# Attentional factorization machine tower on one Trainium2 core: the low part of each step's last chunk made by two DMAs

## The chip, the cores and the metric

The kernel runs on 1 core of one Trainium2 chip. The metric is the device time of one execution in microseconds; the time of a kernel is the median of its runs. Engines are named as in the profile: PE (matmul, with PEld for its weight loads), DVE (vector), ACT (scalar), POOL (GpSimd) and SP (the queue that issues most DMAs). Each engine works off its own instruction stream in order, and semaphores tie the streams together.

## The reference, cut to what matters

```
row, col = np.triu_indices(33, k=1)                      # 528 pairs of 33 fields
e     = stack([tbl_f[ids[:, f]] for f in range(33)], 1)  # (1024, 33, 128)
inner = e[:, row] * e[:, col]                            # (1024, 528, 128)
fm    = relu(einsum('bpd,ad->bpa', inner, attn_W) + attn_b)
scores = einsum('ba,bpa->bp', gnn, fm)
attn   = softmax(scores, axis=1)
pooled = einsum('bp,bpd->bd', attn, inner) * 100.0
h = concat([gnn, pooled, gnn], axis=1)
y = relu(relu(h @ W_top1 + b_top1) @ W_top2 + b_top2) @ W_top3
```

All of it is float32.

## The kernel before, in words

The 1024 samples are worked off in 8 tiles (T) of 128. A tile is 32 steps (STEPS) of 4 samples; a step S, of 256 in all (ALL), has 4 x 528 = 2112 columns (COLS) of products, with the 128 embedding dimensions on the partitions.

For every step DVE forms the products of the field pairs (`product`, L405, tile `inner`), and PE multiplies them by the attention weights (`hidden`, L534 to L543) into PSUM in 5 chunks of 416 or 424 columns. A chunk is done in one of two ways. A native chunk (L534) is a float32 matmul, which runs as two passes. A split chunk takes three matmuls in the faster format float32r: ACT has rounded the products (`round_inner`, L298, `inner_hi`), DVE has subtracted the rounded from the exact ones (`rest_of_inner`, L412, `inner_lo`), and PE adds up low weights times high products, high weights times low products, high weights times high products (L541 to L543). The list NATIVE says how many of a step's chunks, from the first on, are native: 2 in steps 2, 5, 8, 11, 14 and 17 of each tile, 1 in the others, 4 and 3 in the first two steps of all.

ACT adds the bias and applies the relu while it takes two chunks at a time out of PSUM (`relu`, L290, `fm`). After every even step PE turns the two steps before into scores (`reduce_steps`, L564). `inner` and `inner_hi` have three buffers, `inner_lo` two, and PSUM gives three double banks to a ring (`ring`) that all units of PE's work share.

Other work of a tile lies between the steps, at places written out by hand: row maximum, exponential, scaling and transposing of the attention weights of the tile before (steps 1 to 4: L426, L305, L313, L439); the weighted sum over pairs in four parts c = 0 to 3 at steps 7, 10, 13 and 16 (FIELDS_AT; `fields`, L592, then `weigh` L447 and `sum_weighted` L454 on DVE); the transposes of the next tile's embedding rows at steps 18, 20, 22, 24 and 26 (XT_AT; `transpose_x`, L574, taken out of PSUM by ACT, L328); the three layers at steps 19, 21 and 23 (MLP_AT).

POOL gathers the embedding rows, one indirect DMA for each of 33 fields and tile (L259), as soon as the last tile's rows have been transposed and stored. SP stores a tile's rows in DRAM (`store_rows`, L213), and for each part c loads them back turned, with fields on the partitions (`load_fields`, L202, 4 DMAs into `x_fields`), and spreads the attention weights into a block diagonal (`spread_attn`, L207, 4 DMAs into `attn_t`); both tiles have two buffers, so that part c + 1 is loaded while part c is used. In the last tile ACT and DVE spread the weights themselves and parts 2 and 3 have buffers of their own.

These lines tie the low part to its buffers: PE waits for it once in a step, and DVE's product waits until it has been taken.

```
dve.wait_ge(s_lo, S - INNER_BUFS + 1)                                         # product
dve.wait_ge(s_hidden, CHUNKS * (S - INNER_BUFS) + NATIVE[S - INNER_BUFS])     # product
dve.wait_ge(s_hidden, CHUNKS * (S - LO_BUFS + 1))                             # rest_of_inner
pe.wait_ge(s_lo, S + 1)                                                       # hidden, first split chunk
```

Of the kernel before, what the change touches and what calls it, by code (L numbers as in the profile page):

```python
# [12 lines left out]
def afm_tower(nc, gnn, ids, tables, w1, b1, w2, b2, w3, attn_w, attn_b, out):  # L13
    P = 128
# [30 lines left out]
    SPLIT = COLS - THIN  # L45
    INNER_BUFS, HI_BUFS, LO_BUFS, FM_BUFS = 3, 3, 2, 3
    RING = 3
# [4 lines left out]
    MAX_AT, EXP_AT, INV_AT, SCALE_AT, TURN_AT = 1, 2, 2, 3, 4  # L52
# [21 lines left out]
    with ctx:  # L74
# [13 lines left out]
        inner_hi = sb("inner_hi", [D, HI_BUFS, SPLIT], FP32R)  # L88
        inner_lo = sb("inner_lo", [D, LO_BUFS, SPLIT], FP32R)
# [4 lines left out]
        x_fields = sb("x_fields", [P, 2, FN, D])  # L94
# [3 lines left out]
        attn_t = sb("attn_t", [P, 2, QS, FN, I])  # L98
# [7 lines left out]
        attn_wt_lo = sb("attn_wt_lo", [D, P], FP32R)  # L106
# [3 lines left out]
        h1 = sb("h1", [P, M1, P])  # L110
        h2 = sb("h2", [P, M2, P])
        y_row = sb("y_row", [1, P])
# [6 lines left out]
        gnn_rows = x_fields[:, 0, 0:T, :]  # L119
        attn_w_rows = x_fields[:, 1, 0, :]  # L120
        weighted = attn[:].rearrange("p a b -> p (a b)").rearrange("p (b f) -> p b f", f=I)
        TAIL_INNER = (ALL - 3) % INNER_BUFS
        attn_t_tail = inner[:, TAIL_INNER, 0:2 * QS * FN * I].rearrange("p (c q n i) -> p c q n i", c=2, q=QS, n=FN)
        x_fields_tail = x_rows[:, 0:2 * FN, :].rearrange("p (c n) d -> p c n d", c=2)
# [10 lines left out]
        s_fields = [sem(f"fields_loaded{i}") for i in range(2)]  # L135
# [6 lines left out]
        s_setup = sem("setup_copied")  # L142
        s_blocks = sem("gnn_blocks_written")
        s_inner = sem("inner_ready")
        s_hi = sem("inner_hi_ready")
        s_lo = sem("inner_lo_ready")
        s_hidden = sem("hidden_ready")
# [7 lines left out]
        s_spread = [sem(f"attn_t_written{i}") for i in range(2)]  # L155
        s_tail_zero = sem("tail_attn_t_zeroed")
        s_tail_attn = sem("tail_attn_t_written")
# [39 lines left out]
        def _(sp):  # L197
# [6 lines left out]
            def spread_attn(c):  # L204
                for q in range(QS):
                    own = slice(q * I, (q + 1) * I)
                    sp.dma_start(attn_t[own, c % 2, q], attn_turned[own, c * FN:(c + 1) * FN, :])\  # L207
                        .then_inc(s_spread[c % 2], 16)
# [17 lines left out]
            store_rows(1)  # L226
            sp.wait_ge(s_setup_t, 2)
            sp.wait_ge(s_store, 16)
            load_fields(0, 0, x_fields[:, 0], s_fields[0])
            load_fields(0, 1, x_fields[:, 1], s_fields[1])  # L230
            for t in range(T - 1):
                sp.wait_ge(s_inv, 3 * (t + 1))
                spread_attn(0)
                spread_attn(1)
                for c in (2, 3):
                    sp.wait_ge(s_fields_done, FJ * t + c - 1)
                    load_fields(t, c, x_fields[:, c % 2], s_fields[c % 2])
                    spread_attn(c)
                if t + 2 < T:
                    store_rows(t + 2)  # L240
                sp.wait_ge(s_store, 16 * (t + 2))
                for c in (0, 1):
                    sp.wait_ge(s_fields_done, FJ * t + c + 3)
                    load_fields(t + 1, c, x_fields[:, c], s_fields[c])
            sp.wait_ge(s_store, 16 * T)
            sp.wait_ge(s_xt_done, XJ * T)
# [5 lines left out]
        def _(pool):  # L252
# [17 lines left out]
            for t in range(T):  # L270
                gather(t)
# [406 lines left out]
```

## Time and profile before

| | |
|---|---|
| median of 3 runs | 1276.63 us (1275.88 to 1276.68) |
| the profiled execution | 1274.65 us |
| its span, first to last instruction | 1272.7 us |
| mean granted TensorE clock | 0.999 |
| DMA, over the span | 58.47 MB, 46 GB/s |

The profile is of one execution. A busy share is the time in which an engine had an instruction running, over the span. Matmuls are pipelined, so the lengths of single matmuls overlap; the time from the start of one block to the start of the same block two steps later is the better measure of PE's pace. The number behind `<-` in a row names what ended the idle time ahead of the instruction.

### The profile page before, as it was taken

The numbers are of one execution on the slowest core, as the hardware profiler recorded it, in microseconds if no ns is written. First come the engines' busy times: TensorE is split into PE (matmuls) and PEld (weight loads), VectorE is DVE, ScalarE is ACT, GpSimd is POOL, SyncE is SP. The second block draws the span as 40 slices with busy tenths as digits, with TensorE's granted clock in tenths as the row PEclk, the third lists the DMA queues.
The fourth block names the chain that finished last, engine by engine and source line by source line (L and its number), as shares of the span: only waits on it lengthen the run. The fifth ranks groups of instructions, "written<-read, shape, count | busy, mean of one in ns | idle before, by whom it ended". The sixth has DMA issues, their size and how long they took to land.

```text
span 1272.7 us, 21264 instructions
## 1 busy us (share of the span) xinstructions
PE 1208.2 (95%) x8752; PEld 903.2 (71%) x8752; DVE 1150.1 (90%) x643; ACT 1045.2 (82%) x1038; POOL 473.1 (37%) x271
## 2 busy tenths in 40 slices
PE   1499999999999999999999999999999999999998
PEld 1277776777777777777767777677776777677777
DVE  2499899998999989998999989999899998999974
ACT  2388999789887898879987799878988799887882
POOL 6586784018810487006840088202880000000000
PEclk9999999999999999999999999999999999999999
DMA  4212310311103101131102211031111300012100
GB/s 105 101 35 81 72 31 26 110 38 28 33 27 115 32 26 30 30 107 37 30 23 73 77 30 30 20 110 41 28 34 32 106 18 1 1 30 59 29 1 1
DMA packets 54288, 58.47 MB, mean 46 GB/s; under 512 B 10537, under 2 KB 48561, under 8 KB 53169
## 3 DMA queue, kind: packets, MB, share of 16 engines
q1 hardware_dynamic: 45728, 39.81, 10.5%
q0 software_dynamic: 8448, 17.32, 5.2%
q8 instruction: 69, 1.13, 0.4%
q14 instruction: 27, 0.21, 0.1%
q10 hardware_dynamic: 16, 0.00, 0.0%
HBM read 36.12 MB, written 17.31 MB: 42 GB/s over the span
## 4 chain that ended last, share of the span: by engine, by line
PE 77%; ACT 7%; issue 7%; DVE 6%; POOL 2%; DMA 0%; DVEq 0%; ACTq 0%; POOLq 0%
PE scores L564 18%; PE ring L534 16%; PE ring L541 12%; PE ring L542 11%; PE ring L543 11%; ACT fm L290 3%; PE ring L592 3%; DVE inner L405 3%; ACT inner_hi L298 3%; POOL x_rows L259 2%; PE ring L574 2%; DVE inner_lo L412 2%; PE ring L610 1%; DVE attn L447 1%; PE scores L621 1%
## 5 line engine op out<-in xcount | busy, mean ns | idle before, releaser
L290 ACT ACTIVATE fm<-ring,attn_b_sb 128x848 f32<-128x848 f32 (+1 forms) x640 | 597.3, 972 | 158.5 <-PE ring L534 152.2
L405 DVE TENSOR_TENSOR inner<-xt 128x2112 f32<-128x2112 f32 x256 | 602.2, 2353 | 64.9 <-ACT xt L328 35.1
L259 POOL DMA_INDIRECT x_rows<-in_tbl,ids_all x264 | 470.6, 1782 | 484.3 <-PE ring L574 394.5
L412 DVE TENSOR_TENSOR inner_lo<-inner,inner_hi 128x1688 fp32r<-128x1688 f32 (+4 forms) x256 | 466.8, 1823 | 26.1 <-ACT inner_hi L298 22.9
L541 PE MATMUL ring<-inner_hi,attn_wt_lo 128*128 128x424 f32 (+1 forms) x971 | 434.2, 447 | 4.7 <-ACT fm L290 4.0
L298 ACT CAST inner_hi<-inner 128x1688 fp32r<-128x1688 f32 (+4 forms) x256 | 392.4, 1533 | 5.2 <-DVE inner L405 5.2
L542 PE MATMUL ring<-inner_lo,attn_wt_hi 128*128 128x424 f32 (+1 forms) x971 | 344.1, 354 | 0.0
L543 PE MATMUL ring<-inner_hi,attn_wt_hi 128*128 128x424 f32 (+1 forms) x971 | 344.1, 354 | 0.0
L534 PE MATMUL ring<-inner,attn_wt 128*128 128x424 f32 (+1 forms) x618 | 275.6, 542 | 8.2 <-issue 4.5
L564 PE MATMUL scores<-fm,gnn_blocks 128*32 128x264 f32 x4096 | 254.6, 389 | 5.5 <-ACT exp_pairs L305 5.5
L541 PEld LDWEIGHTS ring<-inner_hi,attn_wt_lo 128*128 128x128 f32 x971 | 182.7, 188 | 72.4 <-issue 38.8
L542 PEld LDWEIGHTS ring<-inner_lo,attn_wt_hi 128*128 128x128 f32 x971 | 183.2, 189 | 43.3 <-issue 40.1
L564 PEld LDWEIGHTS scores<-fm,gnn_blocks 128*32 128x32 f32 x4096 | 119.9, 109 | 107.2 <-ACT fm L290 14.2
L543 PEld LDWEIGHTS ring<-inner_hi,attn_wt_hi 128*128 128x128 f32 x971 | 182.4, 188 | 5.4
L534 PEld LDWEIGHTS ring<-inner,attn_wt 128*128 128x128 f32 x618 | 104.6, 190 | 83.4 <-issue 74.7
L274 POOL MEMSET inner<- 128x2048 f32 x1 | 1.8, 1815 | 276.3 <-PE ring L543 276.3
L328 ACT COPY xt<-ring 128x1024 f32<-128x1024 f32 (+1 forms) x40 | 67.4, 1690 | 25.8 <-PE ring L574 25.8
L574 PE MATMUL ring<-ident,x_rows 128*128 128x128 f32 x264 | 39.2, 292 | 34.4 <-DMA x_rows<-in_tbl,ids_all 31.6
L574 PEld LDWEIGHTS ring<-ident,x_rows 128*128 128x128 f32 x264 | 33.0, 151 | 40.0 <-DMA x_rows<-in_tbl,ids_all 25.7
L592 PE MATMUL ring<-attn_t,x_fields 128*128 128x128 f32 x480 | 58.2, 275 | 0.0
L592 PEld LDWEIGHTS ring<-attn_t,x_fields 128*128 128x128 f32 x480 | 58.0, 191 | 0.3
L447 DVE TENSOR_TENSOR attn<-ring,xt 128x1024 f32<-128x1024 f32 x32 | 38.9, 1216 | 3.6 <-PE ring L592 3.3
(50 smaller groups left out, 253.2 us busy)
## 6 DMA issues: line engine op xcount, KB each, us to landing
x_dram<-x_rows SPq DMA_DIRECT2D x8, 2112.0 KB, 6.6
x_fields<-x_dram SPq DMA_DIRECT2D x120, 128.0 KB, 3.0
x_rows<-in_tbl,ids_all POOLq DMA_INDIRECT x264, 3.4
attn_t<-attn_turned SPq DMA_DIRECT2D x112, 32.0 KB, 1.9
w_sb<-in_W_top SPq DMA_DIRECT2D x2, 512.0 KB, 5.9
x_rows<-x_dram SPq DMA_DIRECT2D x8, 128.0 KB, 4.1
x_fields<-in_r_gnn_feature SPq DMA_DIRECT2D x1, 512.0 KB, 4.0
h<-in_W_top SPq DMA_DIRECT2D x1, 256.0 KB, 6.2
```

The costliest lines, as they stand in the source:

```text
L259: nc.gpsimd.indirect_dma_start(out=x_rows[:, f, :], out_offset=None, in_=tables[f], in_offset=bass.IndirectOffsetOnAxis(ap=ids_all[:, t, f ...
L290: nc.scalar.activation(dst, slot(("hidden", pair, j))[:, :, 0:n], ACT.Relu, bias=attn_b_sb[:, 0:1]).then_inc(s_fm, 1)
L298: nc.scalar.copy(inner_hi[:, S % HI_BUFS, 0:COLS - at], inner[:, S % INNER_BUFS, at:]).then_inc(s_hi, 1)
L405: nc.vector.tensor_tensor(dst, a, b, ALU.mult).then_inc(s_inner, 1)
L412: nc.vector.tensor_tensor(inner_lo[:, S % LO_BUFS, 0:COLS - at], inner[:, S % INNER_BUFS, at:], inner_hi[:, S % HI_BUFS, 0:COLS - at].bitc ...
L534: nc.tensor.matmul(dst, attn_wt[:], inner[:, S % INNER_BUFS, begin:end], start=True, stop=True)\
L541: nc.tensor.matmul(dst, attn_wt_lo[:], hi, start=True, stop=False)
L542: nc.tensor.matmul(dst, attn_wt_hi[:], lo, start=False, stop=False)
L543: nc.tensor.matmul(dst, attn_wt_hi[:], hi, start=False, stop=True).then_inc(s_hidden, 1)
L564: last = nc.tensor.matmul(scores[I * j:I * j + I, h, 0:HALF], block_of(s, j), fm[:, S % FM_BUFS, at:at + HALF], start=s == 0, stop=s == ST ...
L574: last = nc.tensor.transpose(to[:, n // 4, n % 4 * P:(n % 4 + 1) * P], x_rows[:, FU * c + n, :], ident[:])
L592: last = nc.tensor.matmul(bank[:, h, to:to + QS * I], x[:, n, :], own[:, :, n, :], start=True, stop=True)
```

## The change

The low part of the last chunk of each step (columns 1696 or 1688 to 2112) is no longer subtracted on DVE. SP copies these columns of the product into a tile of its own, `inner_lo_dma` with three buffers, and POOL issues a second DMA that adds the rounded columns onto the copy. For the sum to be the low part, rounding yields the negative of the rounded product (ACT's copy becomes an activation with scale -1), DVE's subtraction becomes an addition, and two of the three weights are negated. PE waits for the added columns ahead of a split last chunk.

The native chunks are dealt out anew: 1 in a step, 0 in steps 20, 22, 24, 26, 28 and 30 of a tile, all 5 in the first two steps of all, which therefore have no rounding and no low part. POOL's gathers for the next tile are dealt out over steps from five before the tile on (one or two in a step), between the additions. SP's work is ordered by step: the copy for step S + 3 comes first, then what is due of stores, spreads and loads. `x_fields` and `attn_t` have one buffer in place of two, so a part's loads are issued once the part before has been used. `h1`, `h2` and `y_row` lie in the tile `attn`. In the last tile the spread weights of all four parts lie in `inner` and the rows of parts 1 to 3 in `x_rows`, loaded from step 18 on.

```diff
-    NATIVE_2 = (2, 5, 8, 11, 14, 17)
-    NATIVE = [2 if S % STEPS in NATIVE_2 else 1 for S in range(ALL)]
-    NATIVE[0], NATIVE[1] = 4, 3
+    NATIVE_0 = (20, 22, 24, 26, 28, 30)
+    NATIVE = [0 if S % STEPS in NATIVE_0 else 1 for S in range(ALL)]
+    FIRST = 2
+    for S in range(FIRST):
+        NATIVE[S] = CHUNKS
+    LAST = CHUNKS - 1
+    DMA_BUFS = 3
+    SPREAD_AT = 5
+    STORE_AT = 18
+    def gathers_of(S):
+        t, s = divmod(S + 5, STEPS)
+        return t + 1, [f for f in range(F) if f * 2 // 3 == s] if t + 1 < T else []
...
+        def split_step(S):
+            return S - FIRST + 1
+        def dma_turn(S):
+            return 16 * len(range(S, FIRST - 1, -DMA_BUFS))
+        def dma_cols(S):
+            return EDGES[S % 2][LAST], EDGES[S % 2][LAST + 1]
...
+            def copy_inner(S):
+                sp.wait_ge(s_inner, S + 1)
+                if S >= FIRST + DMA_BUFS:
+                    sp.wait_ge(s_hidden, CHUNKS * (S - DMA_BUFS + 1))
+                begin, end = dma_cols(S)
+                sp.dma_start(inner_lo_dma[:, S % DMA_BUFS, 0:end - begin].bitcast(FP32),
+                             inner[:, S % INNER_BUFS, begin:end]).then_inc(s_copied[S % DMA_BUFS], 16)
...
+            load_fields(0, 0, x_fields[:], s_fields)
+            copy_inner(FIRST)
+            for S in range(ALL):
+                t, s = divmod(S, STEPS)
+                if S + 3 < ALL:
+                    copy_inner(S + 3)
+                if s == STORE_AT and t + 1 < T:
+                    store_rows(t + 1)
+                if s == SPREAD_AT and t > 0:
+                    sp.wait_ge(s_inv, 3 * t)
+                    spread_attn(0)
+                for c in range(FJ):
+                    if s == FIELDS_AT[c] + 1 and t > 0:
+                        sp.wait_ge(s_fields_done, FJ * (t - 1) + c + 1)
+                        if c + 1 < FJ:
+                            spread_attn(c + 1)
+                            load_fields(t - 1, c + 1, x_fields[:], s_fields)
+                        else:
+                            sp.wait_ge(s_store, 16 * (t + 1))
+                            load_fields(t, 0, x_fields[:], s_fields)
+                if t == T - 1 and s == STORE_AT:
+                    for c in range(1, FJ):
+                        load_fields(T - 1, c, x_fields_tail[:, c], s_fields_tail)
...
+            def take_off_hi(S):
+                pool.wait_ge(s_hi, split_step(S))
+                pool.wait_ge(s_copied[S % DMA_BUFS], dma_turn(S))
+                begin, end = dma_cols(S)
+                nc.gpsimd.dma_start(inner_lo_dma[:, S % DMA_BUFS, 0:end - begin].bitcast(FP32),
+                                    inner_hi[:, S % HI_BUFS, begin:end].bitcast(FP32), accum_op=ALU.add)\
+                    .then_inc(s_added[S % DMA_BUFS], 16)
...
-            for t in range(T):
-                gather(t)
+            for f in range(F):
+                gather(0, f)
+            for S in range(-5, ALL):
+                if 0 <= S and S + 2 < ALL:
+                    take_off_hi(S + 2)
+                t, some = gathers_of(S)
+                for f in some:
+                    gather(t, f)
...
-                nc.scalar.copy(inner_hi[:, S % HI_BUFS, 0:COLS - at], inner[:, S % INNER_BUFS, at:]).then_inc(s_hi, 1)
+                nc.scalar.activation(inner_hi[:, S % HI_BUFS, at:], inner[:, S % INNER_BUFS, at:], ACT.Copy, scale=-1.0)\
+                    .then_inc(s_hi, 1)
...
             def product(S):
+                if S >= FIRST + INNER_BUFS:
+                    dve.wait_ge(s_lo, split_step(S - INNER_BUFS))
+                    dve.wait_ge(s_copied[S % DMA_BUFS], dma_turn(S - INNER_BUFS))
                 if S >= INNER_BUFS:
-                    dve.wait_ge(s_lo, S - INNER_BUFS + 1)
                     dve.wait_ge(s_hidden, CHUNKS * (S - INNER_BUFS) + NATIVE[S - INNER_BUFS])
...
-                at = native_cols(S)
-                nc.vector.tensor_tensor(inner_lo[:, S % LO_BUFS, 0:COLS - at], inner[:, S % INNER_BUFS, at:],
-                                        inner_hi[:, S % HI_BUFS, 0:COLS - at].bitcast(FP32), ALU.subtract).then_inc(s_lo, 1)
+                at, end = native_cols(S), EDGES[S % 2][LAST]
+                nc.vector.tensor_tensor(inner_lo[:, S % LO_BUFS, at:end], inner[:, S % INNER_BUFS, at:end],
+                                        inner_hi[:, S % HI_BUFS, at:end].bitcast(FP32), ALU.add).then_inc(s_lo, 1)
...
+                    if c < LAST:
+                        lo = inner_lo[:, S % LO_BUFS, begin:end]
+                    else:
+                        pe.wait_ge(s_added[S % DMA_BUFS], dma_turn(S))
+                        lo = inner_lo_dma[:, S % DMA_BUFS, 0:end - begin]
+                    nc.tensor.matmul(dst, attn_wt_lo_neg[:], hi, start=True, stop=False)
                     nc.tensor.matmul(dst, attn_wt_hi[:], lo, start=False, stop=False)
+                    nc.tensor.matmul(dst, attn_wt_hi_neg[:], hi, start=False, stop=True).then_inc(s_hidden, 1)
```

## Rows read from the trace of the kernel before

**Rows 1.** The page: busy time, share and instructions of each engine.
```profile
PE 1208.2 (95%) x8752; PEld 903.2 (71%) x8752; DVE 1150.1 (90%) x643; ACT 1045.2 (82%) x1038; POOL 473.1 (37%) x271
L259 POOL DMA_INDIRECT x_rows<-in_tbl,ids_all x264 | 470.6, 1782 | 484.3 <-PE ring L574 394.5
```

**Rows 2.** Windows of tile 3: steps 2-6, 7-17, 18-23; length, then busy us.
```profile
501.04:524.27 23.23, 21.95 (x165) 15.14 (x165) 23.02 (x17) 21.53 (x23) 3.52 (x2) 1.00 0.07 18
524.27:576.47 52.20, 52.12 (x378) 39.80 (x375) 51.53 (x30) 38.44 (x37) 0.00 (x0) 1.00 0.28 88
576.47:609.18 32.71, 31.98 (x242) 24.54 (x240) 28.28 (x16) 32.55 (x35) 24.82 (x12) 1.00 0.09 23
```

**Rows 3.** The chain that ended last, tile 0: starts of the scores blocks, one per pair.
```profile
90.59 1.92 PE scores L564 x32
98.73 1.92 PE scores L564 x32
107.01 1.92 PE scores L564 x32
```

**Rows 4.** Groups by line and shape: busy us, mean ns, idle before.
```profile
L412 DVE TENSOR_TENSOR inner_lo<-inner,inner_hi 128x1696 fp32r<-128x1696 f32 x103 | 197.8, 1921 | 5.4 <-ACT inner_hi L298 2.2
L298 ACT CAST inner_hi<-inner 128x1696 fp32r<-128x1696 f32 x103 | 165.0, 1602 | 0.3 <-DVE inner L405 0.3
L412 DVE TENSOR_TENSOR inner_lo<-inner,inner_hi 128x1272 fp32r<-128x1272 f32 x24 | 35.4, 1475 | 0.0
L298 ACT CAST inner_hi<-inner 128x1272 fp32r<-128x1272 f32 x24 | 29.9, 1248 | 0.0
```

**Rows 5.** Waits over the span: engine, line, releaser, us in total, times, longest.
```profile
PEld ring L541 <- DVE attn L447: 5.5, 14, 0.5
```

**Rows 6.** Timeline of ACT around steps 18 to 23 of tile 3: start, length.
```profile
579.10 1.62 ACT L298 CAST inner_hi<-inner 128x1688 fp32r<-128x1688 f32 x1
...
610.74 0.97 ACT L290 ACTIVATE fm<-ring,attn_b_sb 128x848 f32<-128x848 f32 x1 [0.72 <-PE ring L543]
```

**Rows 7.** POOL's gathers: shortest, median, longest ns; then landing after issue.
```profile
L259 POOL DMA_INDIRECT x_rows<-in_tbl,ids_all x264: 941/1744/3135, 4.6 to 953.8; - x132
...
DMA to landing us min/median/max: 2.4/3.4/4.7
```

**Rows 8.** Timeline of DVE and POOL in tile 1: two gathers beside DVE.
```profile
287.89 2.35 DVE L405 TENSOR_TENSOR inner<-xt 128x2112 f32<-128x2112 f32 x1
289.09 1.96 POOL L259 DMA_INDIRECT x_rows<-in_tbl,ids_all  x1 [0.30 <-issue]
291.35 0.94 POOL L259 DMA_INDIRECT x_rows<-in_tbl,ids_all  x1 [0.30 <-issue]
291.41 1.92 DVE L412 TENSOR_TENSOR inner_lo<-inner,inner_hi 128x1688 fp32r<-128x1688 f32 x1 [1.18 <-ACT inner_hi L298]
```

**Rows 9.** Timeline of the start: PE's first step, POOL's gathers for tile 1.
```profile
53.15 4.99 PE L534 MATMUL ring<-inner,attn_wt 128*128 128x424 f32 x8 [4.51 <-issue]
55.02 1.11 POOL L259 DMA_INDIRECT x_rows<-in_tbl,ids_all  x1 [8.86 <-DMA x_dram<-x_rows]
...
67.71 0.96 PE L534 MATMUL ring<-inner,attn_wt 128*128 128x416 f32 x2
...
70.18 1.53 POOL L259 DMA_INDIRECT x_rows<-in_tbl,ids_all  x1 [0.30 <-issue]
```

**Rows 10.** Windows of the end; the last three columns: clock, DMA, GB/s.
```profile
1242.80:1244.80 2.00, 0.00 (x0) 0.00 (x0) 0.71 (x1) 1.22 (x2) 0.00 (x0) 1.00 0.00 0
1244.80:1248.20 3.40, 3.34 (x8) 2.62 (x9) 2.08 (x3) 1.18 (x3) 0.00 (x0) 0.50 0.00 0
```

**Rows 11.** SP's issues of the spread weights: shortest, median, longest ns.
```profile
L207 SPq DMA_DIRECT2D attn_t<-attn_turned x112: 512/590/1815, 214.1 to 1148.2; - x112
```

**Rows 12.** SP's loads of the field rows: ns of an issue; the page: landing.
```profile
L202 SPq DMA_DIRECT2D x_fields<-x_dram x120: 303/451/1292, 123.5 to 1174.4; - x120
x_fields<-x_dram SPq DMA_DIRECT2D x120, 128.0 KB, 3.0
```

More of the change, by code:

```diff
@@ L116, in afm_tower @@
         inv_sum = sb("inv_sum", [P, 1])
[L119 to L124, printed above, removed]
+        gnn_rows = x_fields[:, 0:T, :]
+        attn_w_rows = attn_turned[:, 0:D // I, :].rearrange("p n i -> p (n i)")
+        spare = attn[:].rearrange("p a b -> p (a b)")
+        weighted = spare.rearrange("p (b f) -> p b f", f=I)
+        h1 = spare[:, 0:H1].rearrange("p (m b) -> p m b", b=P)
+        h2 = spare[:, H1:H1 + H2].rearrange("p (m b) -> p m b", b=P)
+        y_row = spare[0:1, H1 + H2:H1 + H2 + P]
+        assert {S % INNER_BUFS for S in (ALL - 3, ALL - 2)} == {1, 2}
+        attn_t_tail = inner[:, 1:3, :].rearrange("p r n -> p (r n)")[:, 0:FJ * QS * FN * I]\
+            .rearrange("p (c q n i) -> p c q n i", c=FJ, q=QS, n=FN)
+        x_fields_tail = x_rows[:, 0:FJ * FN, :].rearrange("p (c n) d -> p c n d", c=FJ)
         ring = [pb(f"ring{i}", [P, 2, 512]) for i in range(RING)]
@@ L134, in afm_tower @@
         s_store = sem("rows_stored")
-        s_fields = [sem(f"fields_loaded{i}") for i in range(2)]
+        s_fields = sem("fields_loaded")
         s_fields_tail = sem("tail_fields_loaded")
@@ L146, in afm_tower @@
         s_lo = sem("inner_lo_ready")
+        s_copied = [sem(f"inner_copied{i}") for i in range(DMA_BUFS)]
+        s_added = [sem(f"inner_hi_taken_off{i}") for i in range(DMA_BUFS)]
         s_hidden = sem("hidden_ready")
@@ L154, in afm_tower @@
         s_attn = sem("attn_scaled")
-        s_spread = [sem(f"attn_t_written{i}") for i in range(2)]
+        s_spread = sem("attn_t_written")
         s_tail_zero = sem("tail_attn_t_zeroed")
-        s_tail_attn = sem("tail_attn_t_written")
+        s_tail_attn = [sem(f"tail_attn_t_written{i}") for i in range(2)]
         s_fields_done = sem("fields_filled")
@@ L225, in _ @@
             store_rows(0)
-            store_rows(1)
             sp.wait_ge(s_setup_t, 2)
             sp.wait_ge(s_store, 16)
[L229 to L246, printed above, removed]
-            load_fields(T - 1, 2, x_fields_tail[:, 0], s_fields_tail)
-            load_fields(T - 1, 3, x_fields_tail[:, 1], s_fields_tail)
+            load_fields(0, 0, x_fields[:], s_fields)
[21 more added lines that the diff above has]
+                        load_fields(T - 1, c, x_fields_tail[:, c], s_fields_tail)
             sp.wait_ge(s_out, 16 * T)
@@ L349, in _ @@
             nc.scalar.copy(attn_wt_hi[:], attn_wt[:]).then_inc(s_setup, 1)
+            nc.scalar.activation(attn_wt_hi_neg[:], attn_wt[:], ACT.Copy, scale=-1.0).then_inc(s_wt_neg, 1)
             for c in range(XJ):
@@ L476, in _ @@
             product(1)
-            rest_of_inner(0)
             product(2)
```

117 lines of the change are left out of this document (54 added, 63 removed).

## Prediction

> **What bounds the kernel now.** I read the busy shares first, then the stages of one middle tile, then the waits. PE is busy 95% of the span, DVE 90%, ACT 82%, POOL 37% [rows 1]; the reader should see that three engines are close together, so a gain on one is soon met by the next. The windows of tile 3 say where [rows 2]. In steps 7 to 17 (52.20 us) PE works 52.12 and DVE 51.53. In steps 2 to 6 (23.23 us) DVE works 23.02 and PE 21.95. In steps 18 to 23 (32.71 us) ACT works 32.55 and PE 31.98. PE sets the pace nearly everywhere, with ACT equal to it while the next tile is transposed and DVE equal to it early in the tile. What can be won is mostly PE's own work.
>
> **PE: fewer native chunks.** A native chunk is two float32 passes, a split chunk three short ones. The starts of the scores blocks give the price: the pair of steps with two native chunks in all lasted 98.73 - 90.59 = 8.14 us, the next, with three, 107.01 - 98.73 = 8.28 [rows 3]; the pairs on either side repeat these two lengths. One native chunk more costs 0.14 us. Before has 38 native chunks a tile and 5 more in the first two steps, 309; after has 26 a tile and 8 more there, 216. (a) The six second native chunks of a tile go: 48 x 0.14 = -6.7. (b) Six even steps (20 to 30) lose their only one. That takes the change of weights out of the step too, which no row shows; bounds 0.14 and 0.20, I take 0.17. Three of the six lie in the stretch where ACT sets the pace in the tiles that transpose a next one (7 of 8) and give nothing there: 48 - 21 = 27 x 0.17 = -4.6.
>
> **DVE** subtracts 1272 columns in place of 1696 in 20 of 32 steps: 1.92 - 1.47 = 0.45 us each [rows 4], 9 us a tile, and keeps its 2.35 us product [rows 8]. Most of it only turns into idle time, since PE has the same length. What PE waited for DVE's weighting is 5.5 us in 14 waits [rows 5]; with DVE early I take (c) -4.5 (bounds 0 and -5.5).
>
> **ACT** rounds 2112 columns in place of 1696 in the steps 20 to 30 that are even, and 1696 in place of 1272 in the old two-native steps: 1.602 - 1.248 = 0.35 us for each 424 columns [rows 4]. In steps 7 to 17 ACT has gaps that cover it (38.44 us of work in 52.20 [rows 2]), but from step 18 on it has none until 610.7 [rows 6]. Three longer roundings fall in that stretch: up to 1.06 us a tile, less where PE was late as well; (d) 0.5 x 7 = +3.5 (bounds 0 and 7.4). Step 5's longer rounding stands ahead of the scaling of attn, behind which ACT's next two evacuations queue: (e) 7 x 0.35 = +2.5 (bounds 0 and 2.5). Rounding becomes an activation with a scale and the subtraction an addition; same columns, taken at nothing; 0.05 us more for each rounding would be hidden except in the ACT stretch (+0.3 a tile, inside (d)'s bound).
>
> **POOL and the two DMAs.** Per step SP copies 217 KB and POOL issues an accumulating DMA of the same size, 254 each. No row shows an accumulating DMA. The nearest are the gathers: 0.94 us of POOL at least, 1.74 median, 3.14 at most, landing 2.4 to 4.7 us after issue, median 3.4 [rows 7], plus 0.30 us between two. Why they spread is seen in [rows 8]: the gather of 289.09 ended 0.81 us after DVE's product did (287.89 + 2.35 = 290.24; 291.05), while the one of 291.35 took 0.94 although a DVE subtraction of two inputs ran over nearly all of it. So a gather is held once, at its start, while DVE runs; its remaining 0.8 us is not disturbed. A plain DMA has no index list to read, so I take 0.94 + 0.30 = 1.25 us (bounds 0.94 and 3.44) and 3.4 us to land.
> That is weighed against a rule of the Trainium skill. The page "SBUF — State Buffer", section "SBUF: two separate sides", warns that DMAs issued from GpSimd can starve while VectorE holds the shared port pair; it also says that an op with two SBUF inputs holds it only against a GpSimd op that reads SBUF. The row of 291.35 agrees with the second half. If the first half governed here, it would be the rival "POOL" below.
> POOL per pair of steps in the 22 steps with gathers: three gathers at 1.90 + 0.30 (the 231 gathers after the first 33 take 470.6 - 33 x 0.945 = 439 us [rows 1, 7]) and two adds at 1.25: 6.6 + 2.5 = 9.1 us, against 8.14 us for a pair without extra jobs [rows 3]. It fits only because a gather gets through at each of four DVE ends in a pair, and because the add is early: rounding for step S+2 is done 4.25 us after step S begins (579.10 + 1.62 - 576.47) [rows 2, 6], while PE wants the last chunk at 8.14 + 0.73 + 3 x 0.59 = 10.6 us (8.14 less 1.92 for scores leaves 6.2 for ten chunks, two of them native and 0.14 dearer: 0.59 a split one, 0.73 a native one, an estimate). 10.6 - 4.25 - 3.4 leaves 3.0 us, room for a queue of one gather. (f) 0 in the steady tile, 0 to +3 us a tile in the range.
>
> **The start.** POOL's program puts eight gathers of tile 1 ahead of the first add (step 2). They can't start before 55.02, when tile 0's rows are stored, and the same eight ended at 70.18 + 1.53 = 71.7 in the trace [rows 9]. DVE runs out of work there after its sixth product, so I take 70.5, add 1.25 and land at 74.0. PE would ask for that chunk at about 65.1: ten native chunks from 53.15, 10 x 0.73 = 7.3, and 2.1 more because four of them took 4.99 and not 2.9 at the start [rows 9]; then 2.5 for step 2's first four. It waits 8.9 us, and step 3, at 67.71 before [rows 9], begins at 74.0 + 0.6 + 1.9 = 76.5: +8.8. The clock adds to it: after 2.0 us without PE work the granted clock was 0.50 (1.2 GHz) for 3.4 us late in the trace [rows 10]; the half of 3.4 is 1.7. (g) +10.5 (bounds 7.5, a short add and no clock, and 12.5).
>
> **Single buffers.** The fields' loads for part c+1 are issued by SP only after part c is used, behind the step's copy and four spread DMAs at 0.59 us each [rows 11]; four loads at 0.45 follow, the last landing 3.0 us after issue [rows 12]. From the start of step 8: the copy waits for product 11 (3.7), + 0.5 + 2.3 + 1.3 + 3.0 = 10.8; PE wants them at 11.2 (steps 8, 9 and hidden of 10). A near tie, in 21 places: (h) +2.5 (bounds 0 and 10). Behind the late SP stands the next copy; the 3 us above cover it. The tail's copies are fewer before the first part, but the 12 filler matmuls end at the same time: 0.
>
> **Sum.** -6.7 - 4.6 - 4.5 + 3.5 + 2.5 + 0 + 10.5 + 2.5 = +3.2. The profiled execution took 1274.65 (span 1272.7 and 1.95 around it); the median of the three runs is 1276.63, 2 us above. On the median: **1280**.
>
> **Rivals.**
> *POOL becomes the bound (slower).* If the add too is held at its start until DVE ends, a pair needs five DVE ends and has four: 4 x 1.92 + 1.25 = 8.9 us, 0.8 over 8.14, in six pairs without jobs 4.8 us a tile, of which some 2 are covered: 7 x 2.8 = +20 with the sum above, about 1300. The same price holds if the add lands in over 6 us. It decides where POOL's five issues exceed the pair. At 2.2 us for each add they take 11.0 against 9.1 in 11 pairs, and the loss would be over 100 us; DVE's idle time when PE is late speaks against that. For it: no row of an accumulating DMA. Against: the row of 291.35.
> *PE's gain comes through whole (faster).* ACT's longer roundings and the reloads hide (d, e, h at 0), a native chunk at the even steps is worth 0.19 in all 48 places (-9.1), DVE's waits go whole, start +9: -6.7 - 9.1 - 5.5 + 9 = -12.3, about 1264. For it: ACT's shares outside one stretch. Against: [rows 6].
> *The start doesn't stall* would need the add ahead of the gathers; the program's order excludes it.
>
> **Chances.** Forecast 0.45 (own range 1271 to 1288), POOL or a late add 0.30, whole gain 0.25. The forecast's own range splits as 0.08 faster, 0.17 within, 0.20 slower, so: faster by over 0.2% 0.33, within 0.2% 0.17, slower 0.50; 0.2%, 2.6 us, is about what a measurement of this kernel can tell from no change. The range takes the whole-gain case's centre and most of the POOL case: 1264 to 1305.
>
> **What would show it.** Start: step 3 at 75 to 78 us and half clock there; if it stands at 68, (g) is wrong. Adds: POOL busy near 0.95 us each whatever DVE does; lengths like the gathers' make the POOL rival right. PE waiting on the added chunk in steps 27 to 6 means that (f) is wrong; a pair without jobs of 8.14 or less means it is right. Steps 18 to 23 longer than 32.7 confirm (d). PE waiting for x_fields confirms (h).

## The result and the profile after

The changed kernel ("after" below; the kernel before it is "before") takes 1316.75 us, the median of 4 runs (1311.78 to 1318.42), against 1276.66 for the kernel before: a ratio of 1.0308 with an interval of 1.0295 to 1.032. Forecast were 1280 and a range of 1264 to 1305. The direction was right; size and range were wrong. The direction was partly luck: of the +3.2 us forecast, +10.5 was the start, which measured less, and +2.5 the reload of the single buffers, which measured ten times as much. The profiled execution took 1311.78, its span is 1309.9, 37.2 us over the span of before.

The page of after, busy shares, the two kinds of POOL's work and the last-ending chain by line:

```profile
PE 1209.3 (92%) x8845; PEld 916.0 (70%) x8845; DVE 1091.1 (83%) x641; ACT 1074.0 (82%) x1037; POOL 669.2 (51%) x525
...
PE scores L614 15%; PE ring L591 10%; PE ring L592 9%; PE ring L593 9%; PE ring L580 9%; DMA x_fields<-x_dram 5%; PE ring L644 4%; ACT fm L340 4%; SPq L234 4%; DVE inner L455 4%; SPq L229 2%; PE ring L624 2%; ACT inner_hi L348 2%; DMA inner_lo_dma<-inner_hi 1%
...
L303 POOL DMA_DIRECT2D inner_lo_dma<-inner_hi x254 | 236.8, 932 | 515.0 <-ACT inner_hi L348 456.9
L294 POOL DMA_INDIRECT x_rows<-in_tbl,ids_all x264 | 432.0, 1636 | 91.2 <-issue 75.7
```

Against [rows 1], DVE has lost 59 us of work and POOL, the forecast's worry, stands at 51%. PE has as much work as before, in a longer span: it waits. What is new in the chain is a transfer, the field rows (`x_fields`, 5%), and SP's queue at the spread (L234, 4%) and load lines (L229, 2%).

The waits, engine, line and releaser, then us in total, times and the longest:

```profile
PE ring L644 <- DMA x_fields<-x_dram: 19.0, 19, 2.4
DVE attn L497 <- PE ring L644: 16.1, 11, 3.2
...
PE ring L591 <- DMA inner_lo_dma<-inner_hi: 7.8, 4, 5.2
```

PE's weighted sums, 28 in the middle tiles and the last, wait for their field rows 19 times; for a low part made by the DMAs it waits four times in 254.

The windows of tile 3, steps 2 to 6, 7 to 17 and 18 to 23, as in [rows 2]:

```profile
518.60:542.11 23.51, 21.79 (x167) 15.40 (x165) 22.78 (x18) 22.02 (x23) 17.27 (x13) 1.00 0.54 125
542.11:601.05 58.94, 53.70 (x382) 41.89 (x379) 48.76 (x29) 39.61 (x38) 40.68 (x29) 0.97 0.57 136
601.05:634.46 33.41, 32.05 (x243) 24.81 (x242) 26.27 (x16) 33.24 (x35) 5.82 (x7) 1.00 0.55 159
```

The first and last stretch are 0.28 and 0.70 us longer. The middle one, which holds the four weighted sums, is 6.74 longer, and PE's idle part of it went from 0.08 to 5.24. Tile 3 is the longest of tiles 1 to 7; in the others the middle stretch is 1.3 to 3.3 us longer than before. From the starts of PE's first product in each step, the whole 37.2 divides into: tiles 1 to 6, 153.4 to 158.2 us each where before has 150.4, together +25.7; tile 0, 147.8 against 138.9, +8.9; step 0 begins at 55.62 and not 53.15, +2.5; tile 7 +1.8; the tail -1.6.

**The middle stretch.** SP's timeline in steps 14 and 15 of tile 3 (step 14 begins at 578.71), then PE's of step 16: start, length, and in brackets the wait ahead.

```profile
582.43 0.47 SPq L241 DMA_DIRECT2D inner_lo_dma<-inner  x1
582.95 3.46 SPq L234 DMA_DIRECT2D attn_t<-attn_turned  x4
586.45 2.06 SPq L229 DMA_DIRECT2D x_fields<-x_dram  x4
...
589.74 0.34 PE L593 MATMUL ring<-inner_hi,attn_wt_hi_neg 128*128 128x416 f32 x1
592.33 3.61 PE L644 MATMUL ring<-attn_t,x_fields 128*128 128x128 f32 x16 [2.24 <-DMA x_fields<-x_dram]
595.87 1.99 PE L614 MATMUL scores<-fm,gnn_blocks 128*32 128x264 f32 x32
```
```profile
592.33:595.70 3.37, 3.37 (x16) 3.37 (x16) 0.45 (x1) 0.00 (x0) 3.07 (x3) 0.51 0.44 115
```

SP could have reloaded at about 578.9 (in the first experiment the same spread is issued 0.2 us into step 14), but the copy for step 17 is ahead in its queue and waits until 582.43 for DVE's product. The reload's eight issues then end at 588.51, the rows land by 592.33, and PE, ready at 590.1, waits. Step 16 of this tile is the longest of the 21 steps with a reload, 10.93 us for 6.80 before, for two more reasons: one spread issue took 1.55 us, and PE's 16 matmuls behind the wait ran at half pace (3.61 us, 1.95 in the first experiment), at a granted clock of 0.51, the lower of TensorE's two levels (1.2 GHz; the window shown last). In the profile that happened behind one of the 19 waits.

**The start.** PE and POOL around step 2 of tile 0:

```profile
67.47 0.35 PE L593 MATMUL ring<-inner_hi,attn_wt_hi_neg 128*128 128x424 f32 x1
73.07 0.69 PE L591 MATMUL ring<-inner_hi,attn_wt_lo_neg 128*128 128x416 f32 x1 [5.24 <-DMA inner_lo_dma<-inner_hi]
...
74.38 3.17 PE L614 MATMUL scores<-fm,gnn_blocks 128*32 128x264 f32 x32
77.47 0.97 PE L580 MATMUL ring<-inner,attn_wt 128*128 128x416 f32 x2
```
```profile
68.64 1.09 POOL L294 DMA_INDIRECT x_rows<-in_tbl,ids_all  x1 [0.30 <-issue]
69.72 1.01 POOL L303 DMA_DIRECT2D inner_lo_dma<-inner_hi  x1
```
```profile
73.00:76.40 3.40, 3.33 (x23) 1.81 (x27) 1.48 (x1) 0.00 (x0) 2.80 (x3) 0.50 0.64 148
```

The eight gathers end at 69.73, the first addition is issued behind them, PE has it 3.35 us later, and its next work runs at half pace (scores 3.17 against 1.92) at a granted clock of 0.50 (1.2 GHz; the window shown last). Step 3, at 67.71 in [rows 9], begins at 77.47; of these 9.76 us, 2.47 are the later start of step 0 and 7.29 the wait and the half pace.

### The profile page after: what moved, and what is told of

Read it like the earlier page. It is cut to its first block, busy times and chain, and to the rows that moved or that the text cites. A ratio compares the mean times of both kernels' runs of the same rounds, so it can differ in the third digit from the quotient of the medians.

```text
span 1309.9 us, 22775 instructions
## 1 busy us (share of the span) xinstructions
PE 1209.3 (92%) x8845; PEld 916.0 (70%) x8845; DVE 1091.1 (83%) x641; ACT 1074.0 (82%) x1037; POOL 669.2 (51%) x525
## 2 busy tenths in 40 slices
DMA packets 127450, 167.85 MB, mean 128 GB/s; under 512 B 18664, under 2 KB 121712, under 8 KB 126320
## 4 chain that ended last, share of the span: by engine, by line
PE 62%; ACT 9%; DMA 8%; SPq 7%; issue 6%; DVE 5%; another core or an unknown queue 1%; POOL 1%; ACTq 0%; DVEq 0%; POOLq 0%
PE scores L614 15%; PE ring L591 10%; PE ring L592 9%; PE ring L593 9%; PE ring L580 9%; DMA x_fields<-x_dram 5%; PE ring L644 4%; ACT fm L340 4%; SPq L234 4%; DVE inner L455 4%; SPq L229 2%; PE ring L624 2%; ACT inner_hi L348 2%; DMA inner_lo_dma<-inner_hi 1%
## 5 line engine op out<-in xcount | busy, mean ns | idle before, releaser
L303 POOL DMA_DIRECT2D inner_lo_dma<-inner_hi x254 | 236.8, 932 | 515.0 <-ACT inner_hi L348 456.9
L591 PE MATMUL ring<-inner_hi,attn_wt_lo_neg 128*128 128x424 f32 (+1 forms) x1064 | 457.5, 430 | 21.5 <-ACT fm L340 9.7
L462 DVE TENSOR_TENSOR inner_lo<-inner,inner_hi 128x1272 fp32r<-128x1272 f32 (+1 forms) x254 | 397.4, 1564 | 86.5 <-ACT inner_hi L348 77.5
L348 ACT ACTIVATE inner_hi<-inner 128x1688 fp32r<-128x1688 f32 (+1 forms) x254 | 428.7, 1688 | 0.8 <-DVE inner L455 0.8
L593 PE MATMUL ring<-inner_hi,attn_wt_hi_neg 128*128 128x424 f32 (+1 forms) x1064 | 377.1, 354 | 0.0
L592 PE MATMUL ring<-inner_lo,attn_wt_hi 128*128 128x424 f32 x810 | 287.8, 355 | 0.0
L591 PEld LDWEIGHTS ring<-inner_hi,attn_wt_lo_neg 128*128 128x128 f32 x1064 | 200.3, 188 | 92.4 <-issue 43.8
L580 PE MATMUL ring<-inner,attn_wt 128*128 128x416 f32 (+1 forms) x432 | 200.9, 551 | 7.4 <-issue 7.4
L593 PEld LDWEIGHTS ring<-inner_hi,attn_wt_hi_neg 128*128 128x128 f32 x1064 | 200.3, 188 | 5.0
L592 PE MATMUL ring<-inner_lo_dma,attn_wt_hi 128*128 128x416 f32 x254 | 89.9, 354 | 0.0
```

The source lines that it names most:

```text
L303: nc.gpsimd.dma_start(inner_lo_dma[:, S % DMA_BUFS, 0:end - begin].bitcast(FP32), inner_hi[:, S % HI_BUFS, begin:end].bitcast(FP32), accum ...
L348: nc.scalar.activation(inner_hi[:, S % HI_BUFS, at:], inner[:, S % INNER_BUFS, at:], ACT.Copy, scale=-1.0)\
L462: nc.vector.tensor_tensor(inner_lo[:, S % LO_BUFS, at:end], inner[:, S % INNER_BUFS, at:end], inner_hi[:, S % HI_BUFS, at:end].bitcast(FP3 ...
L580: nc.tensor.matmul(dst, attn_wt[:], inner[:, S % INNER_BUFS, begin:end], start=True, stop=True)\
L591: nc.tensor.matmul(dst, attn_wt_lo_neg[:], hi, start=True, stop=False)
L592: nc.tensor.matmul(dst, attn_wt_hi[:], lo, start=False, stop=False)
```

## The experiments

The theory after the result, "queue place": the reload is late because SP issues it behind a copy that waits for DVE, and the rest of the loss is the start. The rivals: the single buffer by itself, the traffic of the copies and additions, and POOL.

**SP's due reload ahead of the step's copy.**

```diff
-                if S + 3 < ALL:
-                    copy_inner(S + 3)
-                if s == STORE_AT and t + 1 < T:
-                    store_rows(t + 1)
                 if s == SPREAD_AT and t > 0:
...
                             load_fields(t, 0, x_fields[:], s_fields)
+                if S + 3 < ALL:
+                    copy_inner(S + 3)
+                if s == STORE_AT and t + 1 < T:
+                    store_rows(t + 1)
```

> The changed kernel, with SP's work of a step turned round: the spread weights and field rows that are due come ahead of the step's copy, not behind it. Steps 10, 13 and 16 are together 4.0 us longer in a middle tile of the changed kernel than in the kernel before (7.9 for 6.8, 6.3 for 4.9, 8.2 for 6.8). Theory 'queue place' (the loads are late because SP issues them behind a copy that waits 3.7 us for its product): these steps fall back to about 6.8, 4.9 and 6.8, 7 x 4.0 = 28 us less, about 1290 us, and no add comes late, since the copy has room. Rival 'DMA load' (the two new streams of DMAs slow the field rows down wherever they are issued): less than half of it, over 1303 us. Rival 'single buffer' (one buffer is too little whatever the order): the same, over 1303 us.

1290.17 us (1286.66 to 1296.52), ratio 1.0094 (1.0066 to 1.0121). Steps 10, 13 and 16 of tiles 1 to 7 fell to 6.88, 4.90 and 6.88 us, with all copies and additions still there; in after's profile they came to 26.5 more in all. The median fell by 26.6, but that the two agree so closely is chance, since this kernel's executions differ by 9.9 us. Queue place is shown. The profiled execution, the slowest of the four, has losses that nothing had foretold: tile 0 took 3.3 us more than in after, and step 7 of tiles 1 and 2 took 7.7 instead of 4.9. POOL, then DVE, then PE in tile 1:

```profile
231.29 9.35 POOL L294 DMA_INDIRECT x_rows<-in_tbl,ids_all  x1 [0.30 <-issue]
240.59 1.00 POOL L303 DMA_DIRECT2D inner_lo_dma<-inner_hi  x1
```
```profile
230.92 1.48 DVE L462 TENSOR_TENSOR inner_lo<-inner,inner_hi 128x1272 fp32r<-128x1272 f32 x1
232.30 2.37 DVE L455 TENSOR_TENSOR inner<-xt 128x2112 f32<-128x2112 f32 x1
234.56 1.50 DVE L462 TENSOR_TENSOR inner_lo<-inner,inner_hi 128x1272 fp32r<-128x1272 f32 x1
235.95 2.38 DVE L455 TENSOR_TENSOR inner<-xt 128x2112 f32<-128x2112 f32 x1
238.21 1.51 DVE L462 TENSOR_TENSOR inner_lo<-inner,inner_hi 128x1272 fp32r<-128x1272 f32 x1
239.72 2.36 DVE L455 TENSOR_TENSOR inner<-xt 128x2112 f32<-128x2112 f32 x1
```
```profile
243.85 0.46 PE L591 MATMUL ring<-inner_hi,attn_wt_lo_neg 128*128 128x424 f32 x1 [2.54 <-DMA inner_lo_dma<-inner_hi]
```

A gather lay 9.35 us on POOL while DVE went from one two-input instruction to the next without a gap; it ended 0.92 us after the first end behind which DVE's next one did not already overlap (239.72). Other long gathers came free at an end that the next instruction did overlap, so which end frees a gather isn't shown. The addition queued behind it was late, and PE waited. The addition itself took 1.00 us beside the next product.

**The first addition ahead of tile 1's gathers.**

```diff
-                if s == STORE_AT and t + 1 < T:
+                if s == (STORE_AT if t > 0 else 23) and t + 1 < T:
...
                 t, some = gathers_of(S)
+                if S < STEPS - 5:
+                    t, some = 1, [f for f in range(F) if f * 2 // 3 == S]
```

> The changed kernel, with the gathers for tile 1 dealt out from step 0 on (two for each three half steps, as for the other tiles, but five steps later) and tile 1's rows stored at step 23 in place of 18, so that no gather stands ahead of the first addition. Theory 'start' (step 2 waits for the addition that stands behind eight gathers): step 2, 12.64 us in the changed kernel, falls to about 5.5 and step 3 begins 7 us earlier, about 1309 us. Rival: the first addition is late because of the copy or the rounding; step 2 stays over 10 us, 1316 us.

1304.51 us (1302.28 to 1310.29), ratio 1.023 (1.0202 to 1.0258). Step 2 took 5.42 us instead of 12.64 and tile 0 140.07 instead of 147.8. The median is 12.2 us below after's, but its executions, like after's, differ by 7 to 8 us. The profiles say more: step 2 is 7.2 us shorter, step 20 1.1, and tile 0 as a whole 7.7.

**Both edits in one kernel.**

> Both edits. If the two losses are independent: 28 + 7 = 35 us less, about 1282 us, still 5 us over the kernel before, from ACT's longer roundings in steps 18 to 23 (0.7 us a tile), step 4 (0.35 a tile) and a start of step 0 that is 2.5 us later. If they overlap, 1290 or more.

1280.75 us (1278.72 to 1285.5), ratio 1.0036 (1.0019 to 1.0052). Tiles 1 to 6 last 150.3 to 150.7. In these tiles everything else in the change adds up to nearly nothing: before has 150.4. The median is still 3.6 us over the 1277.16 of before beside it.

**The kernel before with single-buffered fields and weights.** No copies, no additions.

```diff
-                    sp.dma_start(attn_t[own, c % 2, q], attn_turned[own, c * FN:(c + 1) * FN, :])\
-                        .then_inc(s_spread[c % 2], 16)
+                    sp.dma_start(attn_t[own, 0, q], attn_turned[own, c * FN:(c + 1) * FN, :])\
+                        .then_inc(s_spread[0], 16)
...
-                spread_attn(1)
-                for c in (2, 3):
-                    sp.wait_ge(s_fields_done, FJ * t + c - 1)
-                    load_fields(t, c, x_fields[:, c % 2], s_fields[c % 2])
+                for c in (1, 2, 3):
+                    sp.wait_ge(s_fields_done, FJ * t + c)
+                    spread_attn(c)
+                    load_fields(t, c, x_fields[:, 0], s_fields[0])
...
```

> The kernel before, with spread weights and field rows in one buffer only: part c + 1 is spread and loaded once part c is used (in the last tile parts 0 and 1 keep their two buffers). SP has no copies here. Theory 'queue place': the loads are issued as soon as part c is done, 8 issues take 4.2 us and the last lands 3 us later, 7.2 us, against some 8 us until the next part (two steps); 0 to 3 us slower, 1277 to 1280 us. Rival 'single buffer': as in the changed kernel, 20 us or more slower, over 1296 us.

1277.66 us (1276.65 to 1278.85), ratio 1.0003 (0.9994 to 1.0013); tiles 150.4 as before. The single buffer alone costs nothing. Its step 0 begins at 55.94, though, so the +2.5 us at the start is not the change's: it came in a kernel that has the old start. Before's profiled execution is the odd one: from first to last instruction it lasts 1272.7 us, the 15 executions of before taken beside this kernel 1274.7 to 1275.4.

**The steps without a native chunk moved out of ACT's full stretch**, on top of both edits.

```diff
-    NATIVE_0 = (20, 22, 24, 26, 28, 30)
+    NATIVE_0 = (6, 8, 12, 14, 26, 28)
```

> Both edits of the run before (reload ahead of the copy, first addition ahead of the gathers; 1280.75 us), and the six steps without a native chunk moved from 20, 22, 24, 26, 28, 30 to 6, 8, 12, 14, 26, 28: as many native chunks, but the longer roundings leave the stretch where ACT has no gap. Theory 'ACT': steps 18 to 23 fall from 33.4 us to about 32.7, as in the kernel before, 7 tiles x 0.7 = 5 us less, about 1276 us. Rival 'PE alone' (it doesn't matter where native chunks go, since PE sets the pace): 1280 to 1281 us.

1271.01 us (1269.35 to 1276.87), ratio 0.996 (0.9945 to 0.9976): it beats both kernels, by 0.4% the kernel before, and 5 us more than expected. (The first four kernels, the next four and the last three were measured apart from each other, with before beside them at 1277.16, 1276.96 and 1277.03.) The windows of tile 3, same steps as above:

```profile
502.28:525.80 23.52, 21.81 (x168) 15.60 (x166) 22.78 (x17) 22.37 (x23) 16.35 (x14) 1.00 0.56 129
525.80:576.89 51.09, 51.09 (x385) 40.84 (x382) 49.82 (x30) 40.69 (x38) 40.71 (x28) 1.00 0.69 162
576.89:609.56 32.67, 31.95 (x241) 24.55 (x241) 25.24 (x16) 32.51 (x35) 7.00 (x8) 1.00 0.52 150
```

The last stretch is back at the 32.7 of [rows 2], and the middle one is 1.1 shorter than before, with PE never idle. ACT's longer roundings cost nothing where ACT has gaps. Step 30, which has its native chunk back, also fell, from 5.26 on average to 5.10.

**Both edits, without the additions.** The low part of the last chunk is left as copied.

```diff
-                    take_off_hi(S + 2)
+                    pool.wait_ge(s_hi, split_step(S + 2))
...
-                        pe.wait_ge(s_added[S % DMA_BUFS], dma_turn(S))
+                        pe.wait_ge(s_copied[S % DMA_BUFS], dma_turn(S))
```

> Both edits of the run before, without POOL's additions: SP still copies, PE takes the copy as it is, so the low part of the last chunk is left unreduced. 54 MB of accumulating transfers and 254 issues on POOL are gone. Theory 'cover' (in the steady tile the additions lie wholly beside other work once the first is early): 1279 to 1281 us, tiles of 150.3 to 150.7 as with them. Rival 'the addition is late at times' or slows other transfers: over 3 us less, under 1278 us.

1276.38 us (1274.97 to 1276.86), ratio 0.999 (0.9981 to 1.0), 4.4 less than with them. So they are not quite covered, against (f). The profiled tiles hardly differ (150.3 to 150.4 against 150.3 to 150.7). What differs in them is step 30, 5.26 us on average with additions and 5.09 without: there PE reaches the last chunk before its addition has landed. Tile 0 is 1.2 us shorter without. The spread of the executions is 1.9 us here and 6.8 with additions; where the rest of the 4.4 lies isn't shown.

**ACT's scaling behind step 3's evacuations**, on the 1271.01 kernel, to win (e) back.

```diff
-                if s == SCALE_AT and t > 0:
-                    scale_attn(t - 1)
                 relu(S // 2, 3 if S % 2 else 1)
                 if S % 2:
                     relu(S // 2, 4)
+                if s == SCALE_AT and t > 0:
+                    scale_attn(t - 1)
```

> The kernel with native chunks moved, and on ACT in step 3 the scaling of attn behind the two relus of the step instead of ahead of them. Step 4 lasts 6.16 us in the changed kernel, 5.81 in the one before, 5.1 in tile 0, where nothing is scaled. Theory 'scaling' (PE waits in step 4 for PSUM banks that ACT empties only after the scaling): step 4 falls to 5.1 to 5.4, 7 x 0.8 = 5.6 us less than the kernel with native chunks moved, about 1270 us. Rival: the scaling then comes late for the turning and spreading of attn, and step 7 waits: the same time or longer.

1294.68 us (1287.36 to 1298.22), ratio 1.0154 (1.0137 to 1.0171): a miss. Step 4 fell from 6.16 to 5.09, but step 5 rose from 3.12 to 5.00 and step 8 from 4.99 to 5.33 on average, 1.1 us a tile lost. And in tile 3 step 12 took 11.85. POOL there, then PE:

```profile
540.30 7.21 POOL L294 DMA_INDIRECT x_rows<-in_tbl,ids_all  x1 [0.30 <-issue]
547.45 1.00 POOL L303 DMA_DIRECT2D inner_lo_dma<-inner_hi  x1
...
550.10 2.82 POOL L294 DMA_INDIRECT x_rows<-in_tbl,ids_all  x1 [0.30 <-issue]
552.90 1.03 POOL L303 DMA_DIRECT2D inner_lo_dma<-inner_hi  x1
```
```profile
558.81 0.69 PE L593 MATMUL ring<-inner_hi,attn_wt_lo_neg 128*128 128x416 f32 x1 [4.39 <-DMA inner_lo_dma<-inner_hi]
```

As in tile 1 of the first experiment, a gather is held and the additions behind it are late. The one that PE waits for is that of 552.90, with a second held gather just ahead of it; it also took 5.9 us to reach PE, where that of 240.59 took 3.3, and why is not shown. That made a new theory, "held gather", for the losses that the steps do not explain.

**Both edits, without either DMA**: DVE makes all low parts, native chunks as in after.

> Both edits of the run before, with the two DMAs undone: DVE makes the low part of all split chunks (1696 columns, 2112 in the six steps without a native chunk), SP keeps the waits of the copies without the copies, POOL only gathers; native chunks as in the changed kernel. Theory 'DVE' (the DMAs pay for the 93 native chunks that went: DVE, 134 us busy in a tile of 150, gets 14 us more and is back at PE's length): tiles of 151 to 155 us, 1285 to 1310 us. Rival 'PE alone' (DVE's relief was worth nothing): tiles of 150.5, 1280 us.

1295.13 us (1294.7 to 1295.62), ratio 1.0143 (1.0126 to 1.016); tiles 153.1. Without the DMAs the same native chunks cost 14.4 us more than with them: DVE is then without a gap (53.37 us of work in the 53.37 of steps 7 to 17), and steps 6, 8 and 14 take 5.9, 6.1 and 5.9 for 5.1, 5.0 and 5.0. It also shows the holding at its largest. The gathers, issue time shortest, median and longest in ns, of this kernel and then of after:

```profile
L290 POOL DMA_INDIRECT x_rows<-in_tbl,ids_all x264: 940/1960/16264, 4.3 to 1069.4; - x132
```
```profile
L294 POOL DMA_INDIRECT x_rows<-in_tbl,ids_all x264: 940/1400/3456, 4.5 to 1059.8; - x132
```

No addition is queued behind them here, and the executions lie within 0.9 us.

**The late scaling without the additions.** The edit is that of the two kernels together.

> The kernel of e7 without POOL's additions (the low part of the last chunk stays the copied product), so that nothing of PE's waits for POOL's queue in the steps. In e7 one gather of tile 3 lay 7.21 us on POOL and the additions behind it came late: PE waited 4.39 us in step 12. Theory 'held gather': e7's loss beyond the profile is such gathers, in other tiles in each execution; without additions 7 tiles at 1.1 us over e5 (150.5 against 149.4) on 1271.0 stay, 1278.7, or up to 4.4 us less, which the additions cost in e3: 1274 to 1279, and its executions lie within 2.5 us of each other. Rival 'ACT': the scaling behind step 3's evacuations makes the loss by itself: about 1288 to 1295.

1279.78 us (1278.01 to 1282.72), ratio 1.0021 (1.0011 to 1.003). Slightly over the range expected; 14.9 us of the loss went with the additions, though the longest gather lay 8.30 us on POOL. ACT as the cause of the large loss has fallen. The spread, 4.7 us, is more than the 2.5 expected. Gathers were still held, eight of them for over 4 us, and in the profile they cost something without any addition behind them: step 17 took 3.84 to 3.91 us in just the four tiles in which a gather of step 16 lay 4.7 us on POOL, and 3.27 in the others. By which wait is open.

**The late scaling with plain loads for gathers**, in tiles 1 to 7.

```diff
-                nc.gpsimd.indirect_dma_start(
-                    out=x_rows[:, f, :], out_offset=None, in_=tables[f],
-                    in_offset=bass.IndirectOffsetOnAxis(ap=ids_all[:, t, f:f + 1], axis=0),
-                ).then_inc(s_gather[c], 16)
+                if t == 0:
...
+                else:
+                    nc.gpsimd.dma_start(x_rows[:, f, :], tables[f][0:P, :]).then_inc(s_gather[c], 16)
```

> The kernel of e7 with the gathers of tiles 1 to 7 replaced by plain DMAs of 128 rows of the same table, issued by POOL at the same places (the choice of rows by ids is left out for these tiles). Additions stay. Theory 'held gather': a plain DMA is issued in 0.9 to 1.1 us like the additions, whatever DVE does; none lies over 2 us on POOL, no addition is late, and the time is 1273 to 1279 with executions within 2.5 us. Rival 'additions': the additions or POOL's queue as such are late when DVE is full, whatever kind of DMA stands between them: 1288 to 1295 as in e7. Rival 'ACT': the same 1288 to 1295.

1276.87 us (1275.13 to 1279.52), ratio 0.9999 (0.9989 to 1.0009): 17.8 less than with gathers, with all additions in place. The two groups on POOL, busy us and mean ns:

```profile
L306 POOL DMA_DIRECT2D inner_lo_dma<-inner_hi x254 | 220.2, 868 | 840.3 <-ACT inner_hi L353 654.1
...
L300 POOL DMA_DIRECT2D x_rows<-in_tbl x231 | 173.4, 846 | 2.0 <-issue 1.8
```

The longest of the 231 plain loads lay 0.954 us on POOL. Step 17 is 3.26 to 3.28 in every tile. So it is the gather that is held beside DVE's instructions, not POOL's DMAs as such, and it costs most where an addition stands behind it.

**The 1271.01 kernel with plain loads for gathers.** The same edit.

> The kernel of e5 with the gathers of tiles 1 to 7 replaced by plain DMAs of 128 rows of the same table (the choice of rows by ids is left out for these tiles). Theory 'held gather': e5's executions spread from 1269.35 to 1276.87 because a gather is held in some of them; with plain DMAs they lie within 2.5 us and the median is 1267 to 1270. Rival: the spread comes from the additions or the traffic itself and stays, with a median near 1271.

1269.27 us (1268.84 to 1272.53, 4 runs), ratio 0.9942 (0.9925 to 0.996). 1.7 us less than with gathers: in that kernel held gathers cost little in the median. Their intervals overlap, so this is no more than in line with the theory; a spread of 3.7 us stays, more than the 2.5 expected. Beside it the late scaling alone costs 7.6 us (1276.87), the 1.1 a tile that its steps show.

## Why the prediction was wrong, point by point

**The step that failed is (h), single buffers**: +2.5, with bounds 0 and 10, and it measured 26.5 in the profiles. The mechanism was named (loads behind the copy and the spreads in SP's queue, "a near tie, in 21 places") and the first experiment shows it. Its sum was 10.8 against 11.2 us; the 19 places in which PE waited for the rows measured 11.8 to 14.0, with PE ready at 11.4 to 11.6. The first spread was issued at 4.0 to 4.2, as said. The last load was issued at 8.4 to 8.6 in 15 of the 21 places and at 8.9 to 9.7 in six, where 7.8 was forecast: 24 of after's 112 spread issues took over 0.7 us (8 to 24 in the kernels with additions, 1 to 6 in those without). PE had the rows 3.2 to 4.3 us after that issue, where 3.0 came from a trace with little else on the rings [rows 12]: the DMAs move 58.47 MB in before and 167.85 in after. In the single-buffered kernel without copies and additions the last load of a part landed 3.05 us after issue in the median, in a later kernel that has both (the late scaling with plain loads) 3.4: in line with some 0.4 us from the added DMAs. Together the misses cost 1.3 us on average in each of 21 places. The upper bound failed because it was built on medians: one spread in four at the longest of [rows 11], 1.815 for 0.59, gives 10.8 + 1.2 - 11.2 = 0.8 us, 17 us in 21 places.

**(g), the start**: the mechanism was right, an addition queued behind eight gathers and half pace behind the wait, but +10.5 was too much. Step 3 at 77.47 looks like the 76.5 forecast by luck: step 0 began 2.47 us late, for another reason, and the wait and the half pace made 7.3 us, just under the lower bound of 7.5. What the forecast had not seen is step 20 of tile 0, where PE waits for an addition beside the store of tile 1's rows (2.1 MB, issued at 142.88); the experiment moved that store away as well.

```profile
143.16 0.86 POOL L303 DMA_DIRECT2D inner_lo_dma<-inner_hi  x1 [2.86 <-ACT inner_hi L348]
152.15 0.43 PE L591 MATMUL ring<-inner_hi,attn_wt_lo_neg 128*128 128x416 f32 x1 [1.98 <-DMA inner_lo_dma<-inner_hi]
```

This addition took 9.0 us from its issue to PE.

**Without (g) and (h)** the forecast's sum was -9.8 us, and it did not come either: in tiles 1 to 6 the steps other than 10, 13 and 16 last as long as before, to 0.1 us a tile. This is the second step that failed; the points below divide it.

**(a), (b), (c), PE's gains**: -15.8 us were forecast. (a) and (c) came to about 7 us of the 11.2: steps 5, 8 and 14 shortened by 0.14, 0.38 and 0.50 us, DVE's part of (c) among it; steps 2, 11 and 17 did not move in the tiles that have weighted sums. (b) came to nearly nothing: steps 26 and 28 shortened by 0.08 and 0.07, where 0.17 was taken and 0.14 the lower bound, step 24 by 0.13, and step 30 became 0.23 longer, since its last chunk waits for the addition (5.09 without additions). A scores pair with one native chunk more [rows 3] is not the price of the last one.

**(d), (e), ACT**: +0.5 a tile forecast, 0.7 measured in steps 18 to 23; step 4 is 6.16 and not 5.81, exactly the 0.35 of (e). Both were right. That (d) was avoidable is shown by the moved native chunks.

**(f) and the rival POOL**: after's additions take 0.835 to 1.072 us whatever DVE does, and up to 1.19 in the other kernels. The sign named for (f), a pair without jobs of 8.14 or less, was met by steps 28 and 29 (8.07) and missed by 26 and 27 (8.33) and by 30 and 31 (8.45 for 8.23 before). So the choice of the row of 291.35 in [rows 8] was right, 0 to 3 us a tile held, and the rival's own price did not come. But one step of the working was wrong, that "a gather gets through at each of four DVE ends". In [rows 2] steps 7 to 17 of before hold no gather at all (POOL 0.00, x0) and steps 2 to 6 two; nearly all rows of the gathers were from other stretches, and the change moves most of them into these two, where DVE is fullest in before. In before 211 of 213 held gathers came free at the first end of a DVE instruction, in after 134 of 143, in the kernel in which DVE has no gap 176 of 211, the others at the second to the eighth (held: over 1.3 us on POOL). In after none is held over 3.46 us, and none over 3.20 with the first addition alone put ahead. As soon as the reload was mended, gathers of 4.3 to 9.4 us appeared, in step 5, a stretch in which DVE has as much to do as in after (22.79 us of 23.53 in steps 2 to 6, 22.78 of 23.51 in after); why only then is open. Held gathers make the 15 to 18 us of the late scaling, and may be part of the 4.4 that the additions cost with both queues mended; that was not tried apart.

The Trainium skill, page "SBUF — State Buffer", section "Who interferes with whom", says that a VectorE instruction with two SBUF inputs contends with a GpSimd instruction that reads SBUF. These traces agree: the gather, which takes its row numbers from SBUF, is held and the plain load at the same places is not (up to 7.21 us against 0.954; 16.26 where DVE has no gap). They go further than the page's lock for the length of an instruction, since a train of such instructions kept a gather waiting past up to eight ends. The row of 291.35, which the prediction took for a gather that two inputs don't hold, doesn't show that: this gather began 0.06 us before the subtraction did (291.41).

**The rival "whole gain"** needed (d), (e) and (h) at nothing. With the queues mended and (d) avoided, the change gives -6.0 us (1271.01 against 1276.96 beside it), not -12.3; (e) is still in it.

## What to carry to other kernels

Where a buffer is halved, its reload is only as early as its place in the in-order queue that issues it: put what is due at once ahead of what still waits, and count a near tie at the price of a miss times the places. Before work is moved to another stretch, look whether the rows that price it lie in a stretch with the same engines as full; a count of x0 says that nothing is known there. Behind an instruction that can be held for many microseconds, here an indirect gather, queue nothing that the bounding engine needs soon.

## What the runs showed of the hardware

An accumulating DMA of 128 x 416 or 424 float32 from POOL was issued in 0.84 to 1.19 us in all kernels that have it, beside DVE's instructions too. In after it was in PE's hands 3.35 us after issue at the start and 9.0 us beside the store of 2.1 MB. Indirect gathers of 128 rows take 0.94 us alone and up to 16.26 us beside a DVE without gaps. One SP issue takes 0.45 to 0.6 us, now and then 1.3 to 2.06. PE ran at half pace, at a granted clock of 0.50 and 0.51 (1.2 GHz), after waits of 5.24 and 2.24 us. Step 0's start differs by some 2.5 us between executions of kernels with the same start (53.15, 55.94); why is open.
